# In the sync engine's list, the transfer of the global row maxima stands ahead of the 12 spreads of the second halves

## What is computed

```python
x = x + _layernorm(attn(_layernorm(x)))      # attn: local + global attention, 16 heads of 16
#   local:  windows of 128 tokens;  global: windows of 256 tokens; triangular additive mask
#   scores = q @ k.T * scale + mask;  a = softmax(scores);  out = a @ v
x = x + _layernorm(moe(_layernorm(x)))       # top-1 of 32 experts, capacity 320 tokens each
```

## Time and profile before

| | before |
|---|---|
| median of 3 runs | 1631.32 us (1628.41 to 1633.1) |
| the profiled execution | 1638.02 us |
| its span in the profile | 1636.3 us |
| PE busy in the span | 1510.0 us (92%) |
| DVE, ACT, POOL busy | 1238.9, 913.6, 723.6 us |
| mean granted clock of TensorE | 0.969 of full |

### The profile page before, as it was taken

How to read it: one execution, slowest core, us unless ns; L and a number is a source line. 1 busy time by engine, 2 the same in 40 slices (tenths; PEclk the granted TensorE clock), 3 DMA queues, 4 the chain that set the end, 5 groups by cost and what they waited for, 6 DMA issues and landing times.

```text
span 1636.3 us, 39878 instructions
## 1 busy us (share of the span) xinstructions
PE 1510.0 (92%) x13672; PEld 1095.4 (67%) x13672; DVE 1238.9 (76%) x3785; ACT 913.6 (56%) x1919; POOL 723.6 (44%) x1097
## 2 busy tenths in 40 slices
PE   5799999999999999999999999999999854999993
PEld 3567777777777777777777777777776633777772
DVE  2577888888888888788888888888888642788883
ACT  3256666666666666666666666666666532222220
POOL 2113444444444444444444444444444341466666
PEclk9899999999999999999999999999999976999997
DMA  6887666665666665556665555665555203355540
GB/s 126 159 223 191 109 111 100 109 107 105 108 106 107 107 105 105 101 102 105 106 104 101 102 100 101 107 103 103 101 97 98 79 23 102 121 154 170 180 137 11
DMA packets 253720, 183.56 MB, mean 112 GB/s; under 512 B 29492, under 2 KB 252151, under 8 KB 253518
## 3 DMA queue, kind: packets, MB, share of 16 engines
q1 hardware_dynamic: 232414, 164.49, 52.1%
q10 hardware_dynamic: 14192, 12.79, 2.9%
q0 software_dynamic: 6912, 3.73, 0.8%
HBM read 55.78 MB, written 38.04 MB: 57 GB/s over the span
## 4 chain that ended last, share of the span: by engine, by line
PE 55%; SPq 12%; POOL 10%; issue 7%; DVE 6%; DMA 6%; ACT 1%; ACTq 1%; POOLq 0%; DVEq 0%
SPq L400 12%; PE bank L1288 9%; PE bank L1439 9%; PE bank L1398 8%; DMA stack<-mT 5%; PE bank L1319 5%; PE bank L1257 4%; PE bank L1278 3%; PE bank L1270 3%; PE bank L1254 2%; PE bank L1295 2%; POOL rstd L517 2%; POOL xrow L587 2%; POOL slots_scratch L576 2%; PE bank L1452 2%
## 5 line engine op out<-in xcount | busy, mean ns | idle before, releaser
L922 DVE TENSOR_REDUCE mx<-bank 128x2 f32<-128x512 f32 (+1 forms) x768 | 513.9, 673 | 187.3 <-PE bank L1316 99.2
L688 ACT ACTIVATE pt<-bank 128x512 f32<-128x512 f32 x768 | 449.8, 593 | 262.2 <-PE bank L1257 177.0
L1288 PE MATMUL bank<-xnT,weff 128*128 128x256 f32 x1024 | 256.7, 395 | 7.2 <-DVE rest L906 6.4
L1288 PEld LDWEIGHTS bank<-xnT,weff 128*128 128x128 f32 x1024 | 188.5, 194 | 42.9 <-issue 11.9
L1319 PE MATMUL bank<-stack 96*128 96x256 bf16 x1024 | 197.5, 274 | 5.4 <-DVE mx L922 5.1
L1257 PE MATMUL bank<-stack 100*128 100x128 bf16 x2048 | 198.4, 218 | 0.0
L539 POOL TENSOR_TENSOR parts<-rest,parts 128x512 bf16<-128x512 f32 x128 | 147.1, 1158 | 84.2 <-ACT parts L705 84.2
L554 POOL TENSOR_TENSOR obuf<-obuf,xrow 128x512 f32<-128x512 f32 x32 | 40.6, 1269 | 296.6 <-ACT obuf L730 296.6
L1257 PEld LDWEIGHTS bank<-stack 100*128 100x128 bf16 x2048 | 158.1, 97 | 12.7
L699 ACT ACTIVATE parts<-bank,bqk 128x256 bf16<-128x256 f32 x256 | 107.2, 469 | 103.5 <-PE bank L1288 103.4
L1254 PE MATMUL bank<-tri,identb 128*128 128x256 bf16 x512 | 140.8, 275 | 23.0 <-DMA stack<-mT 21.1
(11 more groups left out here) (153 smaller groups left out, 2720.9 us busy)
## 6 DMA issues: line engine op xcount, KB each, us to landing
stack<-parts SPq DMA_DIRECT2D x768, 64.0 KB, 2.6
stack<-parts SPq DMA_DIRECT2D x378, 128.0 KB, 5.4
slots_scratch<-zeros ACTq DMA_DIRECT2D x16, 650.0 KB, 5.6
xr<-x SPq DMA_DIRECT2D x32, 256.0 KB, 7.9
out<-obuf SPq DMA_DIRECT2D x32, 256.0 KB, 2.2
ew<-w_gate SPq DMA_DIRECT2D x32, 256.0 KB, 3.9
ew<-w_up SPq DMA_DIRECT2D x32, 256.0 KB, 5.2
ew<-w_down SPq DMA_DIRECT2D x32, 256.0 KB, 4.3
```

The lines of the kernel that those rows point to most:

```text
L688: act.activation(pt[:, u % 8, :], S2[u % 2][:, :], ACT.Exp).then_inc(p_ready, 1)
L922: dve.reduce_max(dst, src, AX.X).then_inc(s1_read, 1)
L1288: last = pe.matmul(bank[:, t * WIN:(t + 1) * WIN], weff[:, b, c, qk * D + t * P:qk * D + (t + 1) * P], xnT[:, par, c, :], start=(c == 0), ...
```

## The change

`maxima_in(1, c, par)` moves from behind the 12 spreads of the second halves to in front of them. The same DMAs are issued, with the same waits each, in another order on the same engine.

```diff
             def step(s, par):
                 a, b, c, d, f = stages(s)
                 ahead = back(s, -2)
+                if c:
+                    maxima_in(1, c, par)
                 if b:
 
                     if d:
                         wait_alone(sp, s2_full, nth(d, UNITS, UNITS - 1))
                     spread_global(0, 1, b, 1 - par)
                     spread_global(1, 1, b, 1 - par)
-                if c:
-                    maxima_in(1, c, par)
                 if a and (ahead[0] is not None or ahead[1] < NW):
```

## The result

The changed kernel takes 1607.84 us (median of 6 runs, 1602.78 to 1610.02) against 1632.21 for the kernel before in the same comparison (6 runs, 1628.41 to 1637.99). The ratio is 0.9849, with a 95% interval of 0.983 to 0.9867: 24.4 us or 1.5% less. The forecast was 1606, a gain of 25. The profiled execution took 1606.68 us, with a span of 1604.9.

A forecast was written before the change was run, and what follows sets the result against it. TensorE, nearly full, stalls for the late global maxima transfer; 21.2 + 2.6 + 1.7 + 0.3 + 1.0 = 26.8 us off gives 1611.2 from the profile, 1604.5 from the median; forecast 1606, 8 in 10 within 1600 to 1620.

The forecast's parts named there:

- Term 1: The 27 steady steps from 166.51 to 1230.46: stalls go, down to 38.62 us per step, 21.2 us gained.
- the rule of ring order: Spreads in front make the filling's 5.42 us landing; moved ahead, the transfer gains 2.0 there, not 1.0, total 27.8.
- Term 2: Step at 1269.07: its longest stall goes, 2.6 us, plus 1.7 us of lower clock, bounds 0 and 3.4.
- Term 3: The filling: the stall at 166.51 goes, 0.3 us, and 1.0 us at 127.78, bounds 0 and 2.
- a quarter toward the profile: Whole run: forecast 1606 taken a quarter of the way from 1604.5 (median less gain) to 1611.2 (profile less gain).
- A: Part of the stall stays, by a 5.4 us landing or another engine only just ready: 1610 to 1626; 15%.
- B: Outside the recording the spreads are out before the maxima are ready, so the order is idle: 1626 to 1634; 6%.
- C: Slower: SyncE's blocked list bunches issues, the reload of x lands late for GpSimd's sum L587: 1637 to 1670; 4%.

The follow-up runs named there:

- the half projection: The changed kernel with half of the output projection's contraction left out (2 of its 4 terms): 1552.0 us in a single run, steps of 36.88 us.
- the third chip: Repeats on another chip, single runs: changed kernel 1627.76 us, steps 39.1; kernel before, steps 39.37, 1636.74 us as median of 7. Nine spreads ahead also ran there: 0.9903.
- the three with mixed orders in the filling: Against the kernel before: old order in steps 2 and 3 only, ratio 0.9861; new order in step 2 alone, 1.0032; new order everywhere but step 3, 0.9893.
- the load ahead: The kernel before with the load of x (L422, 256 KB) also issued ahead of the maxima's transfer: 1674.48 us, ratio 1.026.

## Why the prediction was right

**The bound and the wait.** Reading the stall from the distance of the steps, and not from the shares, gave 38.62 as the floor; it is 38.60, and the half projection shows that it is TensorE's own work. Term 1, 21.2 us, measured 21.8. The transfer lands in 2.8 us in its new place, as taken from 1302.33 and not from 122.32; the rule of ring order, weighed beside it, shows nothing for this transfer in the steady steps: 2.8 with 0, 6 or 9 spreads ahead, and 3.24 only behind a load of 256 KB. For the local one something like it shows, see below, and in the filling the global transfer of the fourth step landed after 4.1 us, not 5.42, as the rule would have it (4.0 to 4.5 in the four profiles of the changed kernel, 4.9 and 5.4 in the two of before).

**What the move delays.** In the step at 742 the spreads end at 747.39, 9.9 us after the copy (9.8 predicted), the load follows at once, the store at 748.13, 10.6 us after the copy (10.3), the reload of x at 757.52 (18.9 predicted, 20.0 measured). The local transfer was to be issued on its data as before; in this step it is 0.9 us late, in most others not. ScalarE's L699 still waits for TensorE here, [0.66] and [1.03] as in rows 4. What I did not work out is how long the local transfer takes to land when it stands closer behind 12 spreads of 128 KB and the reload of x. By the semaphore updates it took 4.3 us in the median of the steady steps before and takes 6.9 now, while the spreads themselves hardly changed (the page has 5.8 us for them, 5.4 before); which of the two in front delays it no run separates. It cost nothing in the steady steps, but its data is there only 3.3 us before TensorE's unit 0 (2.1 at least), where it was 6.1.

The prediction named a wait of L699 or L587 for a DMA as a sign that it is wrong. Both came, once each in this profile, in the filling:

```profile
87.77 0.47 ACT L699 ACTIVATE parts<-bank,bqk 128x256 bf16<-128x256 f32 x1 [2.45 <-DMA stack<-parts]
```
```profile
148.00 1.27 POOL L587 TENSOR_TENSOR xrow<-ybuf,xr 128x512 f32<-128x512 f32 x1 [6.05 <-DMA xr<-x]
```

Before, neither waits for a DMA there. L587 waits so in all four profiles of the changed kernel (3.3 to 6.1 us), L699 in three of them. No wait of TensorE follows on L587's. Behind L699's TensorE waits 0.67 us for ScalarE, and 0.84 us less at its next wait.

**The step of the longest stall and behind it.** Term 2, 2.6 and 1.7 of clock: measured 2.8 and 2.9. The clock's part was cut in half for fear of gaps, and was nearly the 3.4 at its upper bound.

**The filling: the step that failed.** Term 3 gave +1.3 us. In the profile this stretch lost 3.3. The stalls of 1.15 and 0.33 that the term counted are gone; what it left out is the local maxima's transfer, with 2.88 us of stall and 1.7 of clock. The prediction asked what the move delays in one steady step only. In the filling SyncE waits 8.0 us (68.9 to 76.8) and then 6.9 (109.6 to 116.5) for the maxima, with no idle time left at the local transfer. The size, 4.6 us of a forecast of 25, is inside the range, and part of it comes and goes with the runs: from the first L1254 to the third it was 78.8 us before, and in the changed kernel 82.1, 77.4 and 78.9; on the third chip 79.2 and 82.6.

**From the profile to the median.** The two profiles differ by 31.4 us and the medians by 24.4. The first 6.3 of the profile's lie ahead of the first L1254, and much of them is chance. Already the local transfer of the second step, which no order touches, is issued 2.5 us earlier (62.42 and 59.89). Then a stretch of 6.8 us at the lower clock stands at 73 to 74 us in some kernels of either order (before, the changed kernel's third profile, six spreads ahead, and two of the three with mixed orders in the filling) and not in others (the changed kernel's first two, the third with mixed orders, the half projection, the load ahead, nine spreads ahead; on the third chip 3.4 us at 75.6 to 75.8 in both orders); it costs up to 3.4 us. A part may still be the order's: the first L1254 stands at 81.4 to 86.3 us in the seven profiles in which the transfer of the third step stands first, and at 85.3 to 91.6 in the six others. No run separates the two.

My reason to move the forecast by a quarter toward the profile has nothing to rest on: in the nine comparisons with several runs the profiled run lies between 1.5 us below and 3.1 above the median, 1.2 below in the changed kernel. That 1606 and 1607.84 lie so close is luck in part. Without the first term the profiles differ by 25.1 us where the sum said 26.8: the filling fell 4.6 us short of its term, and the rest of the kernel made up 2.9 of that.

**The rivals.** A, another engine just ready, did not happen in the comparison and did on the third chip: 39.1 us steps, two thirds of the gain of a step gone, and 9 us less instead of 24 in the one run there. I had put it at 15% as a matter of the kernel; it is a matter of the chip as well. B is out by the 0.9849. C: in the step at 742 the reload of x has 9.6 us from issue to L587 (757.52 to 767.15) where 11.8 were predicted, and lands after 6.4 of them; in the steady steps it has 2.8 us in hand in the median and 1.6 at least, where the prediction had 3.9 and 2.6. It is waited for only in the filling. The bunching did not make its landing longer (7.8 us in the median, 8.1 before), so the cost that C feared stayed away; the pushed list cost TensorE time only in the filling.

## What to carry to other kernels

A transfer in a hand-written list has a due time: read when its data is ready, when its reader wants it and how long it takes to land, and put it no earlier than the difference asks. Here six or nine issues could as well stay ahead of it, with the local transfer issued on its data in the filling; that this also saves time was not shown. What a removed stall is worth is read from the distance between steps with and without it, not from the idle time alone; and check the filling by itself, for there the list may have no pause in which a delay ends. A gain of 0.8 us a step that ends where the next engine is just ready can be 0.3 on the next chip.

## What the runs showed of the hardware

The issue of a DMA on ScalarE gets slower while SyncE issues too. In the third step ScalarE still has weights to issue before its first exponential. In the kernel before, SyncE issues 24 spreads meanwhile; in the changed one it pauses from 68.9 us on.

```profile
72.47 0.60 ACTq L645 DMA_DIRECT2D gamma_row<-gamma  x1
73.11 0.62 ACTq L646 DMA_DIRECT2D beta_row<-beta  x1
73.75 0.61 ACTq L647 DMA_DIRECT2D wr<-w_router  x1
```
```profile
69.63 0.45 ACTq L645 DMA_DIRECT2D gamma_row<-gamma  x1
70.10 0.45 ACTq L646 DMA_DIRECT2D beta_row<-beta  x1
70.58 0.46 ACTq L647 DMA_DIRECT2D wr<-w_router  x1
```

The first three rows are of before, the others of after. In all 13 profiles these three issues take 0.45 to 0.46 us where the transfer of step 2 stands first, and 0.59 to 0.63 where it stands behind 6, 9 or 12 spreads. TensorE, which waited 3.26 us for the first exponentials before, waits 0.6 for the local transfer and 2.0 for them in the changed kernel: some 0.7 us less waiting, which the prediction had not looked for.

The granted clock falls at short stalls of an otherwise full TensorE: at one of 1.15 us before the change, and at eight of 0.9 to 2.2 us in the kernel with the load ahead, but not at another of 2.25. It can't be counted per stall; it makes a late transfer dearer than its lateness.
